# A clear of 256 columns on GpSimd in front of every row scatter of a two-layer recurrent and attention kernel with two expert layers

## The reference

```python
xn = _layernorm(x)
s = _L0_attn_ref(xn, ...)        # recurrent scan over 256 steps (a GRU and an SSM), batch 16
g = _silu(_L0_ffn_ref(xn, ...))  # 8 experts 128 -> 512 -> 128, top 2, capacity 1.25
x = x + s * g
xn = _layernorm(x)
s = _L1_attn_ref(xn, ...)        # 16 heads of 64, softmax attention within a sequence
g = _silu(_L1_ffn_ref(xn, ...))  # 160 experts 128 -> 64 -> 128, top 8, and a shared one
x = x + s * g
```

## Time and profile before

| | |
|---|---|
| time before, median of 3 runs | 2086.22 us (2082.82 to 2088.34) |
| profiled execution, its own time | 2083.28 us |
| span of the profiled execution | 2081.5 us |
| granted TensorE clock, mean of the span | 0.938 |
| instructions | 49942 |
| POOL: indirect DMAs of layer 0's scatter (L445) | 64 |
| POOL: indirect DMAs of layer 1's scatter (L469) | 256 |
| the experts' second weights, line 392 | 5120 KB, 15.2 us to landing |

### The profile page before, as it was taken

The page is one execution under the profiler, slowest core; times in us unless marked ns, Lnnn a source line. Parts: engine busy times, 40 slices in busy tenths (PEclk is TensorE's granted clock), DMA queues, the critical chain, the costliest instruction groups (busy, mean ns, idle before and its releaser), DMA issues.

```text
span 2081.5 us, 49942 instructions
## 1 busy us (share of the span) xinstructions
PE 1823.4 (88%) x14389; PEld 1623.3 (78%) x14390; DVE 1272.7 (61%) x4624; ACT 888.1 (43%) x2899; POOL 625.7 (30%) x661
## 2 busy tenths in 40 slices
PE   4699999999999999369999999688888988888786
PEld 2467999999997777239999998677777788787785
DVE  4444444544554434888888888344444677777776
ACT  2212444444442211316666665344444555555453
POOL 0074000000006400016677773000000555555551
PEclk9799999999999975669999999899999999999997
DMA  9511011111001100301111112444444211111111
GB/s 377 238 47 37 23 36 35 36 44 40 25 26 47 30 0 0 159 9 48 48 49 52 51 50 101 147 141 149 149 145 141 58 40 39 38 40 40 38 40 54
DMA packets 153497, 149.29 MB, mean 72 GB/s; under 512 B 16931, under 2 KB 134374, under 8 KB 153062
## 3 DMA queue, kind: packets, MB, share of 16 engines
q1 hardware_dynamic: 130820, 100.98, 14.6%
q0 software_dynamic: 21760, 46.18, 7.5%
q10 hardware_dynamic: 866, 1.51, 0.2%
HBM read 70.95 MB, written 77.66 MB: 71 GB/s over the span
## 4 chain that ended last, share of the span: by engine, by line
PE 67%; DMA 11%; DVE 10%; issue 8%; ACT 2%; POOL 1%; DVEq 1%; ACTq 0%; POOLq 0%; SPq 0%
DMA rows_g<-ys_dram,slot 10%; PE ps_y L735 8%; PE ps_t L940 5%; PE ps_up L1042 5%; PE ps_y L793 4%; PE ps_up L784 4%; PE ps_t L1053 4%; PE ps_up L916 4%; PE ps_y L929 3%; PE ps_t L753 3%; PE ps_t L751 3%; PE ps_rec L750 3%; PE ps_rec L748 3%; PE ps_rec L884 2%; PE ps_rec L1020 2%
## 5 line engine op out<-in xcount | busy, mean ns | idle before, releaser
L479 POOL DMA_INDIRECT rows_g<-ys_dram,slot x256 | 242.7, 948 | 529.8 <-DMA ys_dram<-slots_y 346.7
L623 ACT ACTIVATE probs<-ps_up,negmax 128x256 f32<-128x256 f32 x512 | 240.5, 483 | 323.9 <-DVE negmax L1447 323.9
L469 POOL DMA_INDIRECT xs_dram<-xn_tok,slot x256 | 249.4, 974 | 314.6 <-DVE slot L1349 215.1
L940 PE MATMUL ps_t<-v_sb,probsT 128*128 128x64 f32 x2048 | 261.2, 271 | 2.1 <-DVE ctx_sb L1430 1.5
L940 PEld LDWEIGHTS ps_t<-v_sb,probsT 128*128 128x128 f32 x2048 | 252.7, 194 | 4.3 <-issue 4.2
L735 PE MATMUL ps_y<-zeros 128*128 128x512 bf16 x752 | 219.8, 382 | 0.0
L1206 DVE SCALAR_TENSOR_TENSOR mixn<-ps_rec,cols_sb,th_r 128x16 f32<-128x16 f32 x256 | 59.8, 234 | 245.1 <-PE ps_rec L750 143.1
L1447 DVE TENSOR_REDUCE negmax<-ps_up 128x2 f32<-128x512 f32 x256 | 164.7, 685 | 31.2 <-PE ps_up L916 30.9
L916 PE MATMUL ps_up<-kT,qT 64*128 64x256 f32 x1536 | 127.7, 299 | 60.6 <-DVE kT L1403 60.0
L916 PEld LDWEIGHTS ps_up<-kT,qT 64*128 64x128 f32 x1536 | 101.7, 190 | 81.2 <-issue 60.8
L929 PE MATMUL ps_y<-misc,probs 128*128 128x128 f32 x1024 | 163.7, 283 | 0.6 <-ACT probs L623 0.5
(11 more groups left out here) (241 smaller groups left out, 4386.0 us busy)
## 6 DMA issues: line engine op xcount, KB each, us to landing
xs_dram<-zeros SPq DMA_DIRECT2D x52, 512.0 KB, 9.3
slots_x<-xs_dram SPq DMA_DIRECT2D x88, 256.0 KB, 3.0
ys_dram<-slots_y SPq DMA_DIRECT2D x84, 256.0 KB, 2.5
slots_x<-xs_dram SPq DMA_DIRECT2D x41, 128.0 KB, 2.1
ys_dram<-slots_y SPq DMA_DIRECT2D x40, 128.0 KB, 1.8
gate<-w_gate SPq DMA_DIRECT2D x1, 5120.0 KB, 20.7
down<-w_down SPq DMA_DIRECT2D x1, 5120.0 KB, 15.2
w_sb<-w POOLq DMA_DIRECT2D x16, 256.0 KB, 4.8
```

Of the source, the lines that this page charges most:

```text
L469: nc.gpsimd.indirect_dma_start(xs_dram, bass.IndirectOffsetOnAxis(ap=slot[:, n, k:k + 1], axis=0), xn_tok[:, n, :], None).then_inc(scatter ...
L479: nc.gpsimd.indirect_dma_start(rows_g[:, i % 16, :], None, ys_dram, bass.IndirectOffsetOnAxis(ap=slot[:, i // TOPK1, i % TOPK1:i % TOPK1 + ...
L623: nc.scalar.activation(probs[:, a, i, :], ps_s[a][:, T * i:T * i + T], ACT.Exp, bias=negmax[:, a, i:i + 1], accum_out=sums[:, j % 4, i, a: ...
L940: last = nc.tensor.matmul(ps_ctx[:, P * i + HD * a:P * i + HD * a + HD], probsT[:, a, kc, P * i:P * i + P], v_sb[:, j % 2, kc, HD * a:HD * ...
```

## The change

In front of each scatter POOL writes zeros over 256 columns of a buffer that nobody uses at that time, and waits until this is done; then it issues the scatter. In layer 0 the buffer is `slots0_y`, in layer 1 it is `small[:, 1792:2048]`. DVE waits for the last of the 32 * (2 + 8) = 320 clears before the expert loop of layer 1 in which it writes `own`.

```diff
@@ -239,6 +239,7 @@
         zeros_ready = sem("zeros_ready")
+        paused = sem("paused")
         logits_ready = sem("logits_ready")
@@ -435,6 +436,12 @@
             load_expert(1)
 
+            pauses = Count(paused)
+
+            def rest(where):
+
+                pool.wait_ge(paused, pauses.raised_by(nc.gpsimd.memset(where, 0.0)))
+
             pool.wait_ge(slots0_ready, 1)
@@ -442,6 +449,7 @@
                 for k in range(2):
                     if n:
                         pool.wait_ge(scattered0[k], 16 * n)
+                    rest(slots0_y[:, :, :].rearrange("p s d -> p (s d)"))
                     nc.gpsimd.indirect_dma_start(xs0_dram, bass.IndirectOffsetOnAxis(ap=slot_to[:, n, k:k + 1], axis=0),
                                                  xn_tok[:, n, :], None).then_inc(scattered0[k], 16)
@@ -466,6 +474,7 @@
                     if n or k >= 2:
                         pool.wait_ge(scattered[k % 2], 16 * (n * (TOPK1 // 2) + k // 2))
+                    rest(small[:, 1792:2048])
                     nc.gpsimd.indirect_dma_start(xs_dram, bass.IndirectOffsetOnAxis(ap=slot[:, n, k:k + 1], axis=0),
                                                  xn_tok[:, n, :], None).then_inc(scattered[k % 2], 16)
@@ -1483,6 +1492,7 @@
             dve.sem_inc(y_out[1], 1)
+            dve.wait_ge(paused, NT * (2 + TOPK1))
             with dve.Fori(0, NBODY) as it:
```

## The result

On the chip of the result the changed kernel takes **2147.0 us** (median of 4 runs, 2144.4 to 2151.7), the kernel before 2087.3 (2082.8 to 2092.9): a ratio of **1.029** [1.026, 1.032]. The profiled execution took 2148.0 us, its span is 2146.2, 64.7 more than before.

The account below looks back on a forecast made before the run. POOL's serial order bounds the scatters; each gains 0.41 us, charged beyond slack. Layer 0 adds 5.5, layer 1 adds 71.6 (105.0 - 4 - 24.8 - 4.6): 77.1 on 2083.3 is 2160.4, stated as 2161, range 2118 to 2218.

Parts of the forecast that it names:

- POOL's order as the bound: Scatters in both layers: POOL itself sets the 1.26 us interval, so anything put into its order adds its whole length.
- Landing-bound: Rival, chance 0.10: the landing of the scatter two before sets the pace, 0.205 us added per scatter, 2102 us.
- The clearing's 0.31: POOL's memset of 256 columns in front of each scatter takes 0.31 us, from memsets of 1 and 1024 columns.
- The gap of 0.10 in front of the clearing: On POOL, between a scatter's end and the memset: 0.10 us, chosen between 0 and 0.30.
- The scatter's start-up of 0.30 after any release: On POOL, a scatter pays 0.30 us after any release, so waiting for the memset adds nothing.
- Layer 0: 5.5 us: Before PE's first turn: 64 x 0.41 = 26.2 us less slack 20.7 makes PE wait 5.5 us; bounds 0 and 18.3.
- The slack of 24.8, and 4.6 won behind the load: Layer 1: scatters have 24.8 us before SP's first load needs them; that load then reaches PE's turn 4.6 us faster.
- The 4 us of late landings let go: Layer 1's scatters: longer intervals absorb some waits for late landings, an estimated -4 us.
- The signs named: What would show the forecast right: scatter interval, last scatter starts, SP's waits on landings, PE's idle time before turn and experts.
- Clearings held up by DVE: Rival, chance 0.09: in attention's first half DVE's two-input instructions delay memsets 0.2 us on average, 52 over 256: 2213 us.
- DVE held up by clearings: Rival, chance 0.05: each of layer 0's 40 early steps loses 0.21 us on DVE, PE's turn 8.4 later: 2164 us.
- Under attention PE has no idle time to win: Attention beside layer 1's scatters: no mechanism of size makes the kernel faster; chance of faster 0.01.

Follow-up runs that it names:

- experiment 4: The changed kernel without POOL's wait between clearing and scatter; each clearing waits for the one before it instead: 2118.1 us, ratio 1.015.
- experiment 1: The changed kernel with clearings in layer 0 alone, those of layer 1 taken out: 2088.0 us, ratio 1.000.
- experiment 3: The changed kernel with SP's load of w_down moved behind its wait for the scatters: 2146.4 us, ratio 1.029.

## Why the prediction was right, and where it was not

The forecast was 2161 us in 2118 to 2218, slower at 0.96; the result is 2147.0 and slower. Point by point:

- **POOL's order as the bound.** Right, and its working too: the interval is scatter, clearing, start-up, one after the other. The second scatter of all had shown this. Landing-bound (2102) falls: in front of 244 of 256 clearings POOL waited for no landing, and the 12 waits add up to 24.3 us.
- **The clearing's 0.31.** Measured 0.31 to 0.33 in all but one of layer 1's 256.
- **The gap of 0.10 in front of the clearing.** This is the term that was mis-sized, and nothing in it was measured: it was a choice between two rows. It is 0: the clearing starts where the scatter ends. Of the two bounds the lower was the true one, and the row it came from, small memsets one behind the other without a gap, was the nearer kin: a memset behind something. It took 255 x 0.10 = 25.5 us too many in layer 1 and made the 5.5 of layer 0 out of nothing.
- **The scatter's start-up of 0.30 after any release.** Measured 0.28 behind a waited clearing; experiment 4 shows that it isn't a constant: 0.17 of it stay when the wait goes.
- **Layer 0: 5.5 us.** Wrong by the same gap: 64 x 0.31 = 20 fit into 20.7, and SP still waits 3.7 for PE. The bound of "hidden, 0" was named and held, but for the 1.6 us further on that experiment 1 shows.
- **The slack of 24.8, and 4.6 won behind the load.** Measured 24.4 and 4.9. The reading of two timeline rows carried both.
- **The 4 us of late landings let go.** 4.1 outside the collision. But the forecast let the last quarter of the scatters run into the stretch where the weights are loaded without asking what that does to them, though the earlier trace rows show the DMA share of 0.60 there. That missed term is +11.1.
- **The sum.** 2160.4 - 25.5 - 5.5 + 11.1 = 2140.5 by the corrected terms; the remaining 7.5 up to 2148.0 are the 5.2 upstream (3.6 of them that execution's own), 1.4 at the first clearing, 1.8 after PE's turn, less 0.9 in the other terms. So an error of -31 was partly made up for by +11 and +7.5 that the forecast didn't have. That it came as near as 14 us owes something to luck; that it lies in the range doesn't, since with every missed term left out it would be 2129.4 and with the measured ones it is 2148.
- **The signs named.** The interval came out at 1.57 (named 1.67), the last scatters start at 210.9 and 1364.1 (214 and 1378), SP waits 67.4 us for the last one (75), and PE does not stand in front of the first turn (5 named).
- **DVE and the clearings.** "Clearings held up by DVE" (2213) falls: with line 1377's two-input instructions running beside them all through attention's first half, 255 of 256 clearings last 0.31 to 0.33. The row of the scatters' 0.958 had spoken for this. The Trainium skill ("SBUF — State Buffer", Who interferes with whom) says that a VectorE instruction with two SBUF inputs doesn't contend with a GpSimd one that only writes, and the trace agrees. One clearing did meet DVE's cast of 2048 columns:

```profile
928.37 1.32 POOL L443 MEMSET rows_g<- 128x256 f32 x1 [216.25 <-DVE slot L1358]
929.98 2.67 POOL L478 DMA_INDIRECT xs_dram<-xn_tok,slot  x1 [0.28 <-POOL rows_g L443]
```

It lasted 1.32 instead of 0.33 beside a cast that ran from 928.23 for 1.22, and the next scatter 2.67, beside the subtraction that follows. That the cast held the clearing up fits the exclusive lock of which the same section of the Trainium skill speaks; it happened once. "DVE held up by clearings" (2164) falls too: its rows of omz keep a median of 0.175, as in the earlier trace rows, with one of 0.70.

- **"Under attention PE has no idle time to win", so faster at 0.01.** True of the chip whose trace was read, and false on the second kind, where the change made it 13.5% faster and its variants 1.3% to 16%. No row of the trace of before shows it, since in that trace PE is busy beside the scatters all through the earlier trace rows. The forecast is right for the kind of chip that it was made from; as a statement on the change it is half of the truth.

## What to carry to other kernels

A side engine costs nothing until somebody waits for it: find the semaphore, take the difference between when it is raised and when it is wanted, and charge only what exceeds that; whatever is put into a queue that issues one thing at a time costs its full length, with its own completion wait (here 0.33 of clearing, and 0.28 instead of 0.30 in front of the scatter, 0.11 of which is the wait). When such a stream grows past its cover, look at what it now runs into: here another load of 5 MB cost 11 us, and moving that load only moved the loss. And before a change of pace in a DMA stream is dropped or kept, time it on more than one chip: the same edit was 2.9% slower on one and 13.5% faster on another.

## What was not expected of the hardware

- **Two kinds of chip.** The same kernel takes 2085 to 2087 us (medians) on some and 2564 to 2566 on others; single runs of a kind lie within some 1% of each other.
- **Spacing repairs it.** With every indirect transfer of layer 0 and of layer 1's scatter 1.57 to 1.61 us apart, the second kind takes 2148 us. With both scatters at 1.46 and the gathers at 1.39 it takes 2426, with both at 1.35 2535, and with only the gathers left at 1.39 2217.
- **The start of a scatter depends on what it follows:** 0.30 behind a scatter, 0.28 behind a clearing waited for, 0.17 behind one not waited for.
- **A clearing of GpSimd by width:** 0.11 us for 1 column, 0.22 for 128, 0.33 for 256; the row of 1024 has 0.95.
- **A large load beside single scatters:** the 5 MB of w_down kept the landing of a scatter back so far that POOL stood 5.6, 1.7 and 2.3 us in a row; without the load beside it (experiment 3) first to last start is 9.9 us shorter. The other nine waits for a landing add up to 14.7 us in 434, 7.1 of them in one at 946 us whose cause wasn't looked for.
